# One core: local and global softmax sums as neighbours on TensorE, a fourth add of exponentials on GpSimd, and a new order table

## The chip, the cores and the metric

The kernel runs on one core of a Trainium2 chip. The metric is device time in microseconds, the median of several executions. PE is TensorE (PEld its weight loads), DVE is VectorE, ACT is ScalarE, POOL is GpSimd, SP issues DMAs.

## What is computed

A residual block over x of 2 x 8192 tokens by 512. It is normalised, projected to q, k and v for 16 heads of 32, and each query attends twice: to its local window of 64 keys, and to every 64th key of its batch (128 global keys). The two softmax results are added, projected, normalised and added to x. Then follows a second layer whose 512 x 512 matrix is worked out from a sparse spectrum, normalised and added again.

```python
qkv = (x @ w_qkv).reshape(B, N, 3, H, Dh)
logits = einsum('bnqhd,bnkhd->bhnqk', qb, kn) * scale       # keys of 3 windows around a block
logits = where(valid, logits, NEG)                          # -32 <= key - query <= 31
out_local = einsum('bhnqk,bnkhd->bnqhd', softmax(logits), vn)
lg = einsum('bnhd,bghd->bhng', q, k[:, ::W]) * scale
out_global = einsum('bhng,bghd->bnhd', softmax(lg), v[:, ::W])
out = (out_local + out_global) @ w_out + b_out
x = x + layernorm(out);  x = x + layernorm(real(ifft(fft(layernorm(x)) @ w)) + bias)
```

## The kernel before

The first phase (about a third of the time) makes q, k and v and the second layer's matrix. The second phase is a pipeline of 128 steps. A step `s` is one chunk of 512 queries and one group of four heads, so four steps make a chunk of tokens. In a step PE does, under these names:

- `max` (8 pairs of matmuls, L1111): scores from which DVE takes the row maxima (`maxr`, L1007; joined by `maxc`, L1017 to L1020); ACT fills their PSUM bank again with the mask (`seed`, L962). `mt` (L1121) transposes the maxima, and they go back by DMA as rows of the query stack.
- `loc` (8 pairs, L1133), `last` (L1143, the last 64 keys of the chunk) and `glob` (4, L1152): the scores again with the maxima taken off, into the two banks `ps_sc`; ACT takes their exponentials (L933, L940, L946). POOL masks the local ones in two passes for each of four key tiles (`locm`, L883 and L886), and the last keys' (`lastm`, L889).
- `ol` (L1167, L1170): local exponentials times values, four heads side by side in 32-column tiles of the array, into PSUM bank `ps_os`. `oc` on ACT copies it out.
- `sl` (L1186): the local softmax sums, by a matmul with a matrix of ones. A query column can get keys of two neighbouring tiles, so POOL first adds these where they overlap (`sadd`, L893, three a step), and `sl` runs four groups of four heads: 192 columns, 192 columns (the added ones), 128 columns, and the 64 columns of `p_last` (keys of the next chunk's edge, 64 partitions).
- `sg` (L1192): the global sums into the other half of the rows of `ps_os`; DVE then transposes `ps_os` (`sums`, L1024) and inverts it, and spreads it out (`rloc`, `rglob`, L1033). `pvgo` (L1199): global exponentials times values.
- a share of the chunk's `out` and `ffn` matmuls (L1215) and transposes `tr` (L1224), with their layer norms on DVE and POOL (`rs0` to `rs2`, L875 and L877).

The matmuls with 32-column tiles and the two transposes are plain fp32, the rest is fp32r. Every engine runs its items in program order. That order comes from tables of numbers: item `name` of step `s` stands at `PERIOD * s + offset`, all items are sorted by it, and each engine takes its own in that order, waiting on semaphores. The numbers are no times at run time; only the order that they give counts. ACT's exponential of `loc` waits for `sl` of the step before (`sl_done`), `pvgo` for DVE's transpose (`s_turned`), and the third part of `ol` for the fourth `locm`.

Of the kernel before, what the change touches and what calls it, by code (L numbers as in the profile page):

```python
# [21 lines left out]
F32 = mybir.dt.float32  # L22
# [630 lines left out]
def attention_phase(nc, x, v_d, b_out, b_ffn, common, stacks, out):  # L653

    with ExitStack() as ctx:
# [70 lines left out]
        def at_least(eng, s, n):  # L726
# [3 lines left out]

        PERIOD = 16.5
        STEP = {
            "max": (-24.372, -24.443, -17.457, -16.494, -14.783, -19.669, -14.65, -11.428),
            "maxr": (-22.062, -23.735, -17.887, -15.761, -20.864, -13.317, -12.389, -10.81),
            "seed": (-27.861, -23.856, -15.651, -20.132, -14.487, -12.524, -8.36, -1.966),
            "maxc": (-9.904,),
            "mt": (-8.17,),
            "x_mt": (-7.789,),
            "loc": (0.847, 1.259, 1.445, 5.277, 1.584, 4.812, 10.1, 10.414),
            "x_loc": (5.038, 3.297, 1.239, 4.532, 1.974, 9.777, 3.433, 8.956),  # L740
            "locm": (4.363, 2.995, 7.078, 11.037),
            "sadd": (4.613, 13.682, 11.307),
            "last": (4.882,),
            "x_last": (8.223,),
            "lastm": (5.505,),
            "glob": (6.183, 11.975, 7.166, 13.419),
            "x_glob": (16.404, 10.401, 5.594, 6.424),
            "ol": (14.033, 13.563, 14.113),
            "oc": (16.127,),
            "sl": (17.694,),  # L750
            "sg": (17.911,),
            "sums": (19.618,),
            "pvgo": (21.448,),
            "rglob": (21.162,),
            "ogm": (23.645,),
            "rloc": (20.665,),
            "olm": (21.594,),
            "osum": (25.997,),
        }
        BY_GROUP = {  # L760
            "ot": (50.7, 28.42, 45.746, 14.118),
            "otl": (53.185, 27.844, 37.238, 32.356),
        }
        TILE = {
            "out": (23.041, 21.305, 24.153, 22.556, 32.588, 28.022, 27.217, 27.949, 40.453, 39.05, 41.896, 35.968, 42.451, 45.411, 40.17, 44.177),
            "outa": (24.178, 32.38, 39.666, 46.206),
            "outs": (26.18, 36.087, 43.22, 47.902),
            "rs0": (35.584, 27.466, 50.9, 43.784),
            "x1": (29.059, 37.637, 44.069, 51.019),
            "x1s": (29.855, 37.995, 47.034, 55.156),  # L770
            "rs1": (41.755, 33.697, 51.9, 54.124),
            "x1n": (33.895, 45.165, 52.763, 59.748),
            "tr": (40.996, 48.411, 57.83, 64.768),
            "x_tr": (37.041, 48.379, 57.584, 60.74),
            "trl": (40.961, 48.59, 57.292, 65.635),
            "ffn": (56.275, 51.23, 56.716, 48.902, 58.624, 59.685, 61.157, 58.733, 68.241, 65.46, 73.496, 72.963, 76.644, 79.037, 76.65, 82.47),
            "ffna": (56.181, 63.299, 73.349, 83.836),
            "ffns": (79.299, 67.951, 84.667, 80.943),
            "rs2": (72.875, 81.982, 91.045, 81.147),
            "za": (77.179, 83.469, 93.936, 86.7),  # L780
        }
# [31 lines left out]
        with nc.Block() as block:  # L813
# [53 lines left out]
            def _(pool):  # L867
                for g in range(EARLY, GROUPS):
                    stacks.set_keys(pool, g)

                def rstd(k, c, i):
# [7 lines left out]
                def item(name, s, i):  # L879
# [7 lines left out]
                    if name == "lastm":  # L887
                        pool.wait_ge(sc_exped, unit(s, "last", 0) + 1)
                        pool.affine_select(p_last[:], p_last[:], [[0, 4], [1, WIN]], ALU.is_ge, 0.0,  # L889
                                           base=-1, channel_multiplier=-1).then_inc(last_masked, 1)  # L890
# [29 lines left out]
            def _(act):  # L920
# [6 lines left out]
                def item(name, s, i):  # L927
# [8 lines left out]
                    if name == "x_last":  # L936
                        n = unit(s, "last", 0)
                        act.wait_ge(sc_scored, n + 1)
                        at_least(act, sl_done, s)
                        nc.scalar.activation(p_last[:].rearrange("p h n -> p (h n)"), ps_sc[n % 2][0:WIN, 0:4 * WIN],  # L940
                                             ACT.Exp, scale=SCALE).then_inc(sc_exped, 1)
# [137 lines left out]
            def _(pe):  # L1079
# [22 lines left out]
                def item(name, s, i):  # L1102
# [51 lines left out]
                    if name == "ol":  # L1154
# [3 lines left out]
                        for tile in O_PARTS[i]:  # L1158
# [4 lines left out]
                            for h in range(4):  # L1163
                                rows, head = slice(h * DH, (h + 1) * DH), slice(h * DH, (h + 1) * DH)
                                if tile < 4:
                                    x0, w = (0, P) if tile == 0 else (P * tile - WIN, MW)
                                    last = nc.tensor.matmul(ps_os[rows, x0:x0 + w], vw[s % V_BUFS][:, tile, head], p_loc[:, tile, h, MW - w:MW],  # L1167
                                                            start=tile == 0, stop=False, skip_group_check=True)
                                else:
                                    last = nc.tensor.matmul(ps_os[rows, CHUNK - WIN:CHUNK], vl[s % V_BUFS][:, head], p_last[:, h, :],  # L1170
                                                            start=False, stop=True, skip_group_check=True)
# [92 lines left out]
```

## Time and profile before

| what | before |
|---|---|
| time, median of 3 runs | 3414.16 us (3412.81 to 3414.69) |
| the profiled execution's own time | 3419.38 us |
| its span | 3417.6 us |
| busy PE / DVE / ACT / POOL over the span | 98% / 73% / 58% / 56% |
| mean granted TensorE clock | 0.987 |

The share of busy time is the union of an engine's instructions; a matmul's recorded duration includes its way through the array, so the cost of a matmul is better read as the distance from its start to the start of what follows. DVE and POOL have low averages only because the first phase uses them little.

### The profile page before, as it was taken

The numbers are of one execution on the slowest core, as the hardware profiler recorded it, in microseconds if no ns is written. First come the engines' busy times: TensorE is split into PE (matmuls) and PEld (weight loads), VectorE is DVE, ScalarE is ACT, GpSimd is POOL, SyncE is SP. The second block draws the span as 40 slices with busy tenths as digits, with TensorE's granted clock in tenths as the row PEclk, the third lists the DMA queues.
The fourth block names the chain that finished last, engine by engine and source line by source line (L and its number), as shares of the span: only waits on it lengthen the run. The fifth ranks groups of instructions, "written<-read, shape, count | busy, mean of one in ns | idle before, by whom it ended". The sixth has DMA issues, their size and how long they took to land.

```text
span 3417.6 us, 72834 instructions
## 1 busy us (share of the span) xinstructions
PE 3338.3 (98%) x24916; PEld 2508.1 (73%) x24916; DVE 2491.0 (73%) x4425; ACT 1993.9 (58%) x3876; POOL 1915.6 (56%) x2961
## 2 busy tenths in 40 slices
PE   8999999999999699999999999999999999999997
PEld 6888888888888467777777777777777777777775
DVE  4444544445444578988898888988898889888986
ACT  2222322222222567777777777777777777777772
POOL 0000000000000378888788878888888878887885
PEclk9999999999999689999999999999999999999999
DMA  7778778787788656766667666776676666766651
GB/s 186 234 207 242 220 215 239 209 239 223 207 240 239 140 107 142 161 148 142 142 146 160 138 138 144 165 159 139 142 161 148 142 142 149 159 140 137 144 133 38
DMA packets 538325, 572.77 MB, mean 168 GB/s; under 512 B 55752, under 2 KB 354344, under 8 KB 538024
## 3 DMA queue, kind: packets, MB, share of 16 engines
q1 hardware_dynamic: 457992, 533.97, 62.6%
q10 hardware_dynamic: 79744, 34.70, 5.7%
q8 instruction: 176, 2.88, 0.4%
q14 instruction: 125, 1.02, 0.1%
q0 software_dynamic: 288, 0.20, 0.1%
HBM read 330.98 MB, written 203.23 MB: 156 GB/s over the span
## 4 chain that ended last, share of the span: by engine, by line
PE 58%; DVE 5%; POOL 2%; issue 1%; ACT 1%; ACTq 0%; POOLq 0%; DVEq 0%
PE ps_misc L1215 18%; PE ps_mx L1111 9%; PE ps_sc L1133 7%; PE ps_os L1167 5%; PE ps_os L1186 5%; PE ps_os L1192 4%; PE ps_sc L1152 3%; PE ps_os L1199 3%; PE ps_sc L1224 2%; DVE qk L1007 1%; PE ps_os L1170 1%; DVE bnb L989 1%; DVE r_loc L1033 1%; PE ps_sc L1121 1%; DVE r_glob L1033 1%
## 5 line engine op out<-in xcount | busy, mean ns | idle before, releaser
L1007 DVE TENSOR_REDUCE qk<-ps_mx 128x10 f32<-128x640 f32 x1024 | 809.4, 805 | 130.3 <-PE ps_mx L1111 119.1
L962 ACT ACTIVATE ps_mx<-mask 128x640 f32<-128x640 bf16 x1022 | 715.1, 706 | 124.3 <-DVE qk L1007 113.1
L520 PE MATMUL po<-ht_hi,w_both 128*128 128x512 f32 x2048 | 639.0, 391 | 1.5 <-ACT ht_hi L302 1.5
L933 ACT ACTIVATE qk<-ps_sc 128x384 f32<-128x384 f32 (+1 forms) x1024 | 443.4, 459 | 298.0 <-PE ps_sc L1133 242.6
L520 PEld LDWEIGHTS po<-ht_hi,w_both 128*128 128x128 f32 x2048 | 385.3, 188 | 86.3 <-issue 4.1
L883 POOL TENSOR_SCALAR_AFFINE_SELECT qk<-qk 128x512 f32<-128x512 f32 (+1 forms) x512 | 317.6, 620 | 233.1 <-ACT qk L933 228.0
L520 PE MATMUL po<-ht_lo,w_both 128*128 128x512 f32 x1024 | 399.2, 390 | 0.0
L886 POOL TENSOR_SCALAR_AFFINE_SELECT qk<-qk 128x512 f32<-128x512 f32 x512 | 335.3, 655 | 35.0
L524 PE MATMUL po<-w_both,ht_hi 128*128 128x512 f32 x1024 | 320.6, 389 | 1.3 <-DVE w_both L371 1.3
L946 ACT ACTIVATE v<-ps_sc 128x512 f32<-128x512 f32 x512 | 297.0, 593 | 33.3 <-PE ps_sc L1152 33.3
L893 POOL TENSOR_TENSOR qk<-qk 128x256 f32<-128x256 f32 x384 | 290.8, 767 | 10.7
L333 ACT ACTIVATE o_hi<-po 128x512 fp32r<-128x512 f32 x128 | 71.4, 599 | 351.7 <-PE po L524 238.5
L333 ACT ACTIVATE qk<-po 128x512 fp32r<-128x512 f32 x128 | 71.2, 599 | 350.4 <-PE po L524 142.1
L989 DVE BATCH_NORM_STATS2 bnb<-xb 128x6 f32<-128x512 f32 x384 | 258.9, 674 | 2.3
L439 DVE TENSOR_TENSOR o_lo<-po,o_hi 128x512 fp32r<-128x512 f32 x128 | 81.0, 679 | 244.8 <-ACT o_hi L333 244.8
L273 POOL CAST kg_hi<-o_hi 128x32 f32 (+1 forms) x16 | 8.2, 510 | 429.1 <-DVE o_lo L439 429.1
L439 DVE TENSOR_TENSOR o_lo<-po,qk 128x512 fp32r<-128x512 f32 x128 | 80.5, 677 | 221.2 <-ACT qk L333 221.2
L273 POOL CAST kg_hi<-qk 128x32 f32 (+1 forms) x16 | 8.5, 531 | 414.4 <-DVE o_lo L439 393.3
L1111 PE MATMUL ps_mx<-ks,w_both 97*128 97x320 f32 x1024 | 235.8, 333 | 1.5 <-ACT ps_mx L962 1.4
L877 POOL TENSOR_TENSOR rsb<-veb,mhalf_b 128x1 f32<-128x1 f32 x384 | 219.4, 571 | 31.9
L524 PEld LDWEIGHTS po<-w_both,ht_hi 128*128 128x128 f32 x1024 | 192.2, 188 | 41.6 <-DVE w_both L371 1.7
L1111 PEld LDWEIGHTS ps_mx<-ks,w_both 97*128 97x128 f32 x1024 | 164.3, 192 | 79.1 <-ACT ps_mx L962 56.9
(159 smaller groups left out, 7843.0 us busy)
## 6 DMA issues: line engine op xcount, KB each, us to landing
xb<-in_L_attn_x SPq DMA_DIRECT2D x256, 256.0 KB, 6.3
w_both<-q_hi_d SPq DMA_DIRECT2D x256, 256.0 KB
q_lo_d<-o_lo SPq DMA_DIRECT2D x32, 1024.0 KB, 8.6
k_lo_d<-o_lo SPq DMA_DIRECT2D x32, 1024.0 KB, 10.1
w_both<-q_lo_d SPq DMA_DIRECT2D x128, 256.0 KB
vw<-v_d SPq DMA_DIRECT2D x128, 256.0 KB, 5.0
out<-xb SPq DMA_DIRECT2D x128, 256.0 KB, 3.2
bt<-at ACTq DMA_DIRECT2D x496, 64.0 KB, 6.0
```

The costliest lines, as they stand in the source:

```text
L520: last = nc.tensor.matmul(po[bank(o, u)][:], wa[:, k, o * P:(o + 1) * P], ha[u][:, k, :], start=start, stop=stop)
L524: last = nc.tensor.matmul(po[bank(o, u)][:], ha[u][:, k, t * P:(t + 1) * P], wa[:, k, 2 * D:3 * D], start=start, stop=stop)
L883: pool.affine_select(early, early, [[0, 4], [1, WIN if i == 0 else P]], ALU.is_ge, 0.0, base=WIN - 1 if i == 0 else -1, channel_multiplier ...
L886: pool.affine_select(late, late, [[0, 4], [-1, P]], ALU.is_ge, 0.0, base=0, channel_multiplier=1).then_inc(loc_masked, 1)
L893: pool.tensor_tensor(p_sum[:, i, :, :], p_loc[:, i, :, P:MW], p_loc[:, i + 1, :, 0:WIN], ALU.add).then_inc(s_added, 1)
L933: nc.scalar.activation(p_loc[:, tile, 2 * hp:2 * hp + 2, lo:MW], ps_sc[n % 2][:, 0:2 * MW].rearrange("p (h n) -> p h n", h=2)[:, :, lo:MW] ...
L946: nc.scalar.activation(p_glob[:, i, :], ps_sc[n % 2][:], ACT.Exp, scale=SCALE).then_inc(sc_exped, 1)
L962: nc.scalar.activation(ps_mx[u % 2][:, :, 0:MWG], mask[:, turn:turn + 1, :].to_broadcast([P, 2, MWG]), ACT.Copy).then_inc(seeded, 1)
L989: nc.vector.bn_stats(bn[k][:, i, :], src).then_inc(bn_done[k], 1)
L1007: nc.vector.tensor_reduce(mb[s % 2][:, heads, tile, :], ps_mx[u % 2][:, :, 0:MWG].rearrange("p h (b n) -> p h b n", n=WIN), axis=AX.X, op= ...
L1111: last = nc.tensor.matmul(ps_mx[u % 2][:, n, 0:MWG], qs[g][0:ROWS_MAX, 2 * pair + n, tile * P:(tile + 1) * P], ks[g][0:ROWS_MAX, 2 * pair ...
L1215: last = nc.tensor.matmul(ps_misc[:], pick(a), w[:, k, :], start=k == 0 and n == 0, stop=k == KT - 1 and n == 2)
```

## The change

POOL gets a fourth add a step: the last tile's upper half plus `p_last`. For that `p_last` gets 128 partitions, whose upper 64 are set to zero once, and `p_sum` a fourth block; the small buffers that lay behind it move to a tensor of their own. `sl` becomes two groups of 256 columns (the lower and the upper halves of all four query tiles) and waits for the four adds alone. `sg` stands directly behind `sl`. All numbers of the order table are new; of these a few are shown. (The norms' small buffers are also joined into one tensor, and two reads of `p_last` name its first 64 partitions.)

```diff
--- before.py
+++ after.py
@@ -668,15 +668,15 @@
         qk_rest = qk0[:].rearrange("p a n -> p (a n)")[:, 16 * MW:]
-        p_sum = qk_rest[:, 0:12 * WIN].bitcast(F32).rearrange("p (i h n) -> p i h n", i=3, h=4)
+        p_sum = qk_rest[:, 0:16 * WIN].bitcast(F32).rearrange("p (i h n) -> p i h n", i=4, h=4)
...
-        p_last = sb("p_last", [WIN, 4, WIN], F32)
+        p_last = sb("p_last", [P, 4, WIN], F32)
         blocks, joined = 4 * TILES * (MWG // WIN), 8 * TILES
-        small = qk_rest[:, 12 * WIN:12 * WIN + 2 * (blocks + joined)].bitcast(F32)
+        small = sb("small", [P, 2 * (blocks + joined)], F32)[:]
...
@@ -728,56 +728,56 @@
-        PERIOD = 16.5
+        PERIOD = 16.2
         STEP = {
...
-            "sadd": (4.613, 13.682, 11.307),
+            "sadd": (11.647, 15.853, 15.494, 8.939),
...
-            "sl": (17.694,),
-            "sg": (17.911,),
+            "sl": (17.479,),
...
+            "sg": (17.48,),
...
@@ -867,6 +867,10 @@
                 for g in range(EARLY, GROUPS):
                     stacks.set_keys(pool, g)
+                for g in range(EARLY, GROUPS):
+                    pool.wait_ge(stacks.k_made[g], 1)
+                pool.memset(p_last[WIN:P], 0.0).then_inc(rest_zeroed, 1)
+                pool.wait_ge(rest_zeroed, 1)
@@ -886,11 +890,16 @@
                     if name == "sadd":
-                        pool.wait_ge(loc_masked, 4 * s + i + 2)
-                        pool.tensor_tensor(p_sum[:, i, :, :], p_loc[:, i, :, P:MW], p_loc[:, i + 1, :, 0:WIN], ALU.add).then_inc(s_added, 1)
+                        if i < 3:
+                            pool.wait_ge(loc_masked, 4 * s + i + 2)
+                            pool.tensor_tensor(p_sum[:, i, :, :], p_loc[:, i, :, P:MW], p_loc[:, i + 1, :, 0:WIN], ALU.add).then_inc(s_added, 1)
+                        else:
+                            pool.wait_ge(loc_masked, 4 * s + 4)
+                            pool.wait_ge(last_masked, s + 1)
+                            pool.tensor_tensor(p_sum[:, i, :, :], p_loc[:, i, :, P:MW], p_last[:], ALU.add).then_inc(s_added, 1)
@@ -1167,23 +1176,17 @@
                     if name == "sl":
                         pe.wait_ge(o_copied, s + 1)
-                        pe.wait_ge(s_added, 3 * s + 3)
-                        pe.wait_ge(loc_masked, 4 * s + 4)
-                        pe.wait_ge(last_masked, s + 1)
+                        pe.wait_ge(s_added, 4 * s + 4)
                         halves = ps_os[:].rearrange("p (t b n) -> p t b n", b=2, n=WIN)
-                        for n, (sums, windows) in enumerate(((halves[:, 0:3, 0, :], p_loc[:, 0:3, :, WIN:P]),
-                                                             (halves[:, 0:3, 1, :], p_sum[:]),
-                                                             (ps_os[:, CHUNK - P:CHUNK], p_loc[:, 3, :, WIN:MW]),
-                                                             (ps_os[:, CHUNK - WIN:CHUNK], p_last[:]))):
+                        for n, windows in enumerate((p_loc[:, :, :, WIN:P], p_sum[:])):
                             for h in range(4):
-                                window = windows[:, :, h, :] if len(windows.shape) == 4 else windows[:, h, :]
-                                last = nc.tensor.matmul(sums[h * DH:(h + 1) * DH], ones[0:windows.shape[0], 0, :], window,
+                                last = nc.tensor.matmul(halves[h * DH:(h + 1) * DH, :, n, :], ones[:, 0, :], windows[:, :, h, :],
                                                         start=n == 0, stop=False, skip_group_check=True)
                         last.then_inc(sl_done, 1)
```

On PE, around the sums of one step in the steady part. `ps_os<-qk,ones` is `sl`, `ps_os<-v,ones` is `sg`, `ps_sc<-w_both` is `loc`, `ps_mx` is `max`. Before:

```order
L1111 MATMUL ps_mx<-o_lo,w_both 128x320 x2
L1133 MATMUL ps_sc<-w_both 128x128 x2
L1186 MATMUL ps_os<-qk,ones 32x3x64 x8
L1186 MATMUL ps_os<-qk,ones 32x128 x4
L1186 MATMUL ps_os<-p_last,ones 32x64 x4
L1133 MATMUL ps_sc<-w_both 128x128 x2
L1192 MATMUL ps_os<-v,ones 32x512 x4
L1133 MATMUL ps_sc<-w_both 128x192 x4
```

and of the change:

```order
L1142 MATMUL ps_sc<-w_both,o_lo 128x128 x2
L1189 MATMUL ps_os<-qk,ones 32x4x64 x8
L1195 MATMUL ps_os<-v,ones 32x512 x4
L1142 MATMUL ps_sc<-w_both,o_lo 128x128 x2
L1120 MATMUL ps_mx<-ks,w_both 128x320 x4
L1142 MATMUL ps_sc<-w_both,o_lo 128x192 x4
L1202 MATMUL ps_os<-v,w_both 32x512 x4
```

The pair of `loc` that stood between the two sums now stands behind both, and two pairs of `max` stand between it and the next four `loc`; `pvgo` (the last row) follows these. In all, PE's second phase leaves its fp32 matmuls for fp32r ones 644 times before and 575 times after: 127 fewer through the joined sums, and some 60 more because 60 of the `tr` no longer stand right behind `ol`.

On POOL, in the same kind of step, from the fourth `locm` on (`qk<-qk 128x256` is a `sadd`). Before:

```order
L883 AFFINE_SELECT qk<-qk 128x4x128
L886 AFFINE_SELECT qk<-qk 128x4x128
L893 TENSOR_TENSOR qk<-qk 128x256 x2
L875 TENSOR_SCALAR veb<-mvb 128x1
L877 TENSOR_TENSOR rsb<-veb,mhalf_b 128x1
L904 TENSOR_TENSOR ot_lo<-o_loc,ot_hi 128x512
```

and of the change:

```order
L898 TENSOR_TENSOR qk<-qk 128x256
L887 AFFINE_SELECT qk<-qk 128x4x128
L890 AFFINE_SELECT qk<-qk 128x4x128
L898 TENSOR_TENSOR qk<-qk 128x256
L902 TENSOR_TENSOR qk<-qk,p_last 128x256
L879 TENSOR_SCALAR ln_small<-mvb 128x1
```

Of the two adds behind the fourth mask one now stands ahead of it, and the new one is the last, with `sl` waiting for it.

## Rows read from the trace of the kernel before

**Rows 1.** Windows: busy us (instructions) of PE, PEld, DVE, ACT, POOL; clock; DMA share, GB/s

```profile
2000.00:2500.00 500.00, 497.42 (x4540) 356.96 (x4538) 445.31 (x781) 382.41 (x750) 413.12 (x637) 1.00 0.69 152
```

**Rows 2.** Line L1192 (`sg`): count, duration ns min/median/max, first and last start

```profile
L1192 PE MATMUL ps_os<-v,ones x1024: 592/617/1062, 1161.0 to 3364.4; 128*32 128x512 f32 x171
```

**Rows 3.** Timeline of PE around the sums: start us, duration us

```profile
2010.75 0.56 PE L1111 MATMUL ps_mx<-ks,w_both 97*128 97x320 f32 x2
2011.15 0.40 PE L1215 MATMUL ps_misc<-ht_hi,ot_hi 128*128 128x512 f32 x1
...
2011.84 0.46 PE L1111 MATMUL ps_mx<-ks,w_both 97*128 97x320 f32 x2
2012.14 0.34 PE L1133 MATMUL ps_sc<-w_both,ks 99*128 99x128 f32 x2
2012.41 1.08 PE L1186 MATMUL ps_os<-qk,ones 128*32 128x192 f32 x24
2013.41 0.32 PE L1186 MATMUL ps_os<-p_last,ones 64*32 64x64 f32 x8
2013.66 0.44 PE L1133 MATMUL ps_sc<-w_both,ks 99*128 99x128 f32 x2
2014.03 1.07 PE L1192 MATMUL ps_os<-v,ones 128*32 128x512 f32 x8
2015.02 0.69 PE L1133 MATMUL ps_sc<-w_both,ks 99*128 99x192 f32 x4
2015.56 0.77 PE L1111 MATMUL ps_mx<-ks,w_both 97*128 97x320 f32 x4
```

**Rows 4.** Weight loads of `ol`: the first 24 and the last 8, twice

```profile
2009.01 0.70 PEld L1167 LDWEIGHTS ps_os<-qk,vw 128*32 128x32 f32 x24 [0.27 <-issue]
2010.04 0.16 PEld L1167 LDWEIGHTS ps_os<-qk,vw 128*32 128x32 f32 x8 [0.34 <-POOL qk L886]
...
2061.76 0.70 PEld L1167 LDWEIGHTS ps_os<-qk,vw 128*32 128x32 f32 x24 [0.28 <-issue]
2062.64 0.16 PEld L1167 LDWEIGHTS ps_os<-qk,vw 128*32 128x32 f32 x8 [0.17 <-POOL qk L886]
```

**Rows 5.** Timeline of PE, earlier in the step: among fp32r work, and ahead of `ol`

```profile
2005.62 0.59 PE L1133 MATMUL ps_sc<-w_both,o_lo 99*128 99x192 f32 x4
2006.04 0.41 PE L1215 MATMUL ps_misc<-ht_hi,ot_hi 128*128 128x512 f32 x1
...
2008.16 0.40 PE L1152 MATMUL ps_sc<-w_both,o_lo 99*128 99x512 f32 x1
2008.39 0.46 PE L1111 MATMUL ps_mx<-ks,w_both 97*128 97x320 f32 x2
2008.69 0.39 PE L1152 MATMUL ps_sc<-w_both,o_lo 99*128 99x512 f32 x1
```

**Rows 6.** Timeline of PE, `tr` behind `ol`

```profile
2028.76 0.66 PE L1224 MATMUL ps_sc<-ident,xb 128*128 128x128 f32 x4
2029.17 0.55 PE L1111 MATMUL ps_mx<-w_both 97*128 97x320 f32 x2
2029.56 0.40 PE L1215 MATMUL ps_misc<-ht_hi,w_both 128*128 128x512 f32 x1
```

**Rows 7.** POOL's fourth mask of a step, from the timeline

```profile
2009.36 0.63 POOL L886 TENSOR_SCALAR_AFFINE_SELECT qk<-qk 128x512 f32<-128x512 f32 x1
```

**Rows 8.** Two lines by themselves: duration ns min/median/max

```profile
L893 POOL TENSOR_TENSOR qk<-qk x364: 722/732/1179, 1255.9 to 3353.2; 128x256 f32<-128x256 f32 x182
...
L1072 DVE SCALAR_TENSOR_TENSOR xb<-xb,rsb x120: 705/814/1739, 1297.1 to 3325.3; 128x512 f32<-128x512 f32 x120
```

**Rows 9.** Waits, second phase: total us, times, longest

```profile
PEld ps_os L1167 <- POOL qk L886: 38.1, 118, 0.5
...
PE ps_sc L1121 <- DVE qk L1020: 10.8, 31, 0.7
```

**Rows 10.** DVE's transpose of the sums, from the timeline

```profile
2015.16 0.72 DVE L1024 STREAM_TRANSPOSE r_loc<-ps_os 128x512 f32<-128x512 f32 x1 [0.83 <-PE ps_os L1192]
```

More of the change, by code:

```diff
@@ L690, in attention_phase @@
         mv = [sb(f"mvb{s}", [P, TILES, 2], F32) for s in range(3)]
-        ve = [sb(f"veb{s}", [P, TILES], F32) for s in range(3)]
-        rs = [sb(f"rsb{s}", [P, TILES], F32) for s in range(3)]
-        nm = sb("nmb", [P, TILES], F32)
+        ln_small = sb("ln_small", [P, 7, TILES], F32)
+        ve, rs, nm = [ln_small[:, s, :] for s in range(3)], [ln_small[:, 3 + s, :] for s in range(3)], ln_small[:, 6, :]
         ps_mx = [pb(f"ps_mx{b}", [P, 2, 512]) for b in range(2)]
@@ L729, in at_least @@
                 eng.wait_ge(s, n)
-        PERIOD = 16.5
+        PERIOD = 16.2
         STEP = {
[L733 to L741, printed above, removed]
-            "sadd": (4.613, 13.682, 11.307),
[L743 to L749, printed above, removed]
-            "sl": (17.694,),
-            "sg": (17.911,),
[L752 to L758, printed above, removed]
@@ new lines, in attention_phase @@
+            "max": (-22.973, -23.083, -15.972, -16.628, -14.326, -17.22, -14.155, -11.779),
+            "maxr": (-22.311, -19.382, -16.644, -17.707, -22.258, -13.723, -10.173, -12.806),
+            "seed": (-27.909, -21.612, -13.06, -21.226, -13.222, -10.253, -7.789, -0.058),
+            "maxc": (-9.955,),
+            "mt": (-7.27,),
+            "x_mt": (-6.711,),
+            "loc": (1.266, 2.114, 2.835, 5.662, 1.315, 2.274, 10.719, 10.704),
+            "x_loc": (4.205, 3.241, 3.329, 5.933, 3.897, 15.001, 10.514, 9.508),
@@ new lines, in attention_phase @@
+            "locm": (4.658, 9.475, 5.273, 11.717),
+            "sadd": (11.647, 15.853, 15.494, 8.939),
+            "last": (2.648,),
+            "x_last": (7.09,),
+            "lastm": (9.258,),
+            "glob": (6.857, 14.929, 5.767, 15.117),
+            "x_glob": (14.538, 9.424, 4.656, 7.492),
+            "ol": (15.45, 15.342, 15.601),
+            "oc": (17.408,),
+            "sl": (17.479,),
+            "sums": (18.279,),
+            "pvgo": (18.713,),
+            "rglob": (20.388,),
@@ L759, in attention_phase @@
+            "ogm": (23.319,),
+            "rloc": (18.943,),
+            "olm": (22.597,),
+            "osum": (26.525,),
+            "sg": (17.48,),
         }
         BY_GROUP = {
-            "ot": (50.7, 28.42, 45.746, 14.118),
-            "otl": (53.185, 27.844, 37.238, 32.356),
+            "ot": (51.511, 28.196, 46.751, 18.998),
+            "otl": (50.34, 30.06, 37.661, 32.769),
         }
         TILE = {
-            "out": (23.041, 21.305, 24.153, 22.556, 32.588, 28.022, 27.217, 27.949, 40.453, 39.05, 41.896, 35.968, 42.451, 45.411, 40.17, 44.177),
@@ L766, in attention_phase @@
[L766 to L780, printed above, removed]
+            "out": (23.599, 20.491, 20.183, 22.378, 31.386, 29.662, 27.719, 28.443, 40.447, 38.809, 41.916, 35.438, 46.927, 46.895, 42.657, 38.672),
@@ new lines, in attention_phase @@
+            "outa": (25.391, 29.738, 38.966, 43.469),
+            "outs": (25.573, 34.059, 42.992, 46.239),
+            "rs0": (36.909, 27.655, 49.56, 45.901),
+            "x1": (28.362, 36.683, 46.292, 50.393),
+            "x1s": (30.556, 38.867, 47.116, 58.485),
+            "rs1": (42.62, 33.253, 49.788, 58.943),
+            "x1n": (39.097, 46.871, 52.003, 60.222),
+            "tr": (41.191, 48.251, 57.398, 64.709),
+            "x_tr": (51.385, 41.612, 66.663, 56.474),
+            "trl": (40.997, 49.931, 58.67, 64.968),
@@ L781, in attention_phase @@
+            "ffn": (56.003, 54.903, 48.528, 51.62, 58.747, 60.766, 72.451, 60.681, 71.637, 79.715, 58.873, 70.207, 69.051, 75.721, 76.648, 79.55),
+            "ffna": (58.47, 60.134, 73.868, 78.72),
+            "ffns": (58.962, 69.064, 74.832, 79.36),
+            "rs2": (82.577, 83.188, 80.759, 68.475),
+            "za": (77.293, 86.781, 91.146, 80.599),
         }
@@ L888, in item @@
                         pool.wait_ge(sc_exped, unit(s, "last", 0) + 1)
-                        pool.affine_select(p_last[:], p_last[:], [[0, 4], [1, WIN]], ALU.is_ge, 0.0,
+                        pool.affine_select(p_last[0:WIN], p_last[0:WIN], [[0, 4], [1, WIN]], ALU.is_ge, 0.0,
                                            base=-1, channel_multiplier=-1).then_inc(last_masked, 1)
                     if name == "sadd":
-                        pool.wait_ge(loc_masked, 4 * s + i + 2)
-                        pool.tensor_tensor(p_sum[:, i, :, :], p_loc[:, i, :, P:MW], p_loc[:, i + 1, :, 0:WIN], ALU.add).then_inc(s_added, 1)
+                        if i < 3:
[5 more added lines that the diff above has]
+                            pool.tensor_tensor(p_sum[:, i, :, :], p_loc[:, i, :, P:MW], p_last[:], ALU.add).then_inc(s_added, 1)
                     if name == "olm":
@@ L939, in item @@
                         at_least(act, sl_done, s)
-                        nc.scalar.activation(p_last[:].rearrange("p h n -> p (h n)"), ps_sc[n % 2][0:WIN, 0:4 * WIN],
+                        nc.scalar.activation(p_last[0:WIN].rearrange("p h n -> p (h n)"), ps_sc[n % 2][0:WIN, 0:4 * WIN],
                                              ACT.Exp, scale=SCALE).then_inc(sc_exped, 1)
@@ L1169, in item @@
                                 else:
-                                    last = nc.tensor.matmul(ps_os[rows, CHUNK - WIN:CHUNK], vl[s % V_BUFS][:, head], p_last[:, h, :],
+                                    last = nc.tensor.matmul(ps_os[rows, CHUNK - WIN:CHUNK], vl[s % V_BUFS][:, head], p_last[0:WIN, h, :],
                                                             start=False, stop=True, skip_group_check=True)
```

1 line of the change is left out of this document (added).

## The prediction

> **What bounds the kernel now.** I read the windows first. In a steady stretch of 500 us PE is busy 497.42, DVE 445.31, ACT 382.41 and POOL 413.12, at the full granted clock [rows 1]. So in the second phase PE is the bound, with DVE and POOL not far behind, and every bit of PE time that is taken out should show as long as those two keep up. The length of a step comes from the first and last `sg`: 1024 instructions are 128 steps of 8, and (3364.4 - 1161.0) / 127 = 17.35 us [rows 2].
>
> Next the timeline of PE, read from start to start. Two things are to be seen. First, what each group of `sl` costs: its 24 instructions of 192, 192 and 128 columns (512 in sum) take 2013.41 - 2012.41 = 1.00, and the 8 of `p_last` with only 64 columns take another 0.25 [rows 3]. Second, changing between the 32-column fp32 matmuls and the 128-column fp32r ones costs time on both sides. A pair of `max` takes 0.40 behind such a run and 0.30 elsewhere [rows 3]; four `loc` of 192 columns take 0.54 behind `sg` [rows 3] and 0.42 among fp32r work [rows 5]; a `glob` takes 0.23 in general and 2009.01 - 2008.69 = 0.32 when `ol` follows it [rows 4, 5]. So going in costs about 0.10 and coming out about 0.11.
>
> Last the waits. The fourth part of `ol`'s tiles is regularly held by POOL's fourth mask (38.1 us in 118 times [rows 9]): the mask ends at 2009.36 + 0.63 = 2009.99 and the loads go at 2010.04 [rows 4, 7]. How much of that is real? Tiles of 512 columns stand ahead of it; once it came 0.88 behind `ol`'s start and at other times 1.03 [rows 4], so the true loss is up to 0.15 a step.
>
> **The change part by part.** All terms are us per step, on PE.
>
> 1. The `p_last` group goes: -0.25 [rows 3].
> 2. The remaining two groups have 256 + 256 = 512 columns, as `sl`'s first 24 instructions (1.00) and as `sg` (2015.02 - 2014.03 = 0.99) [rows 3]. But both of these are followed by another shape of tile, and some of the 1.00 is the array running empty. Where 512 columns in the same shape are followed by more of the same, the next can start after 0.88 [rows 4]. With `sg` right behind, I take `sl` at 0.88: -0.12. The bounds are 0 (nothing saved, by `sg`'s row) and 0.15 (the 0.88 was itself cut off by a wait for POOL).
> 3. The pair of `loc` between the sums. It costs 2014.03 - 2013.66 = 0.37 there, while the same pair that only goes in costs 2012.41 - 2012.14 = 0.27 [rows 3]. Now it stands behind both sums and only comes out, so it loses the 0.10 of going in, and the four `loc` that stood behind `sg` lose the 0.12 of coming out (0.54 to 0.42). Together -0.22.
> 4. `tr`. Behind `ol`, it let one exit serve both. 60 of the 128 now stand alone among fp32r work. A pair of `max` behind `tr` takes 2029.56 - 2029.17 = 0.39 [rows 6], against 0.30 undisturbed [rows 3]. So +0.09 x 60 / 128 = +0.04.
> 5. The new add on POOL is like L893: 0.73 in the median, 1.18 at most [rows 8]. POOL's load rises from 413.12 / 500 = 83% to (0.826 x 17.35 + 0.73) / 16.8 = 90%. Not on PE's path if it ends in time. Behind the fourth mask come two adds (1.46). PE meanwhile has the last 192 columns of `ol` (an estimate by the 0.88 for 512 columns, plus an exit: 0.33 + 0.11 = 0.44), 0.25 for `p_last`'s part of it (by `sl`'s like group), two pairs of `max` (0.40 + 0.30) and the pair of `loc` (0.27) [rows 3, 4]: 1.66. So the cover is 0.2 even if the mask ends just in time as now. That the first `sadd` now stands ahead of the mask makes the mask 0.73 later on POOL; three `out` matmuls that in one step of four stood behind `ol` now stand ahead of it, and DVE's norms that POOL waits for stand earlier in the order. I cost term 5 at nothing; if its cover is gone it is up to 0.73 a step.
> 6. `pvgo` waits for DVE's transpose, which starts 0.14 after PE leaves `sg` and takes 0.72 [rows 3, 10]. Between `sg` and `pvgo` there now stand a pair of `loc`, four `max` and four `loc`, 0.27 + 0.61 + 0.42 = 1.30 (the 0.61 an estimate, twice 0.30). 0.4 is left, so nothing. Without this cover PE would stand 0.9 a step.
> 7. The new order elsewhere: PE has the same matmuls otherwise. The start (one memset on POOL) happens once, and the semaphores that `sl` no longer names had been reached: nothing.
>
> The sum is -0.25 - 0.12 - 0.22 + 0.04 = -0.55 a step, or 70 us over 128 steps. The profiled execution took 3419.4 us (span 3417.6 and 1.8 around it), which gives 3349; the median of the runs is 5.2 lower, so in its terms **3344**.
>
> A page has a rule for terms 2 and 3. The Trainium skill, "TensorEngine Tiling (Array Packing)", Key Properties, says that a change of tiling mode, not merely of tile, drains TensorE. By it two drains a step go; without it, terms 2 and 3 would be nothing and the sum 27 us.
>
> **The rivals.**
>
> *The gain is partly given back to waits.* DVE is at 89% and would be at 445.31 / 500 x 17.35 / 16.8 = 92%, POOL at 90%, and each is waited for once or twice a step already: by `ol` [rows 9], and by `mt` (31 waits of up to 0.7 for the joined maxima [rows 9]). Where these loops and not PE set the pace, the matmul saved is idle time gained. For it: the third part of `ol` is held in nearly every step. Against it: the two sums and the `loc` between them lie on that very loop (from mask to `ol` to `sg` to DVE's transpose), so it gets shorter too. If 0.25 of the 0.55 stays lost: 3414 - 38 = 3376.
>
> *The run of fp32 brings nothing.* If the cost of changing is bound to the shapes and not to the neighbours, only terms 1 and 4 are left: 0.21 x 128 = 27 us, 3387. Rows 3 and 5 speak against it in three places.
>
> *Waits vanish too.* If the true loss of up to 0.15 at `ol` [rows 4] and some of that at `mt` go with the new order, another 20 to 25 us: 3320.
>
> *Slower: POOL's last add comes too late for `sl`.* `sl` now waits for a chain mask, add, add. L893 can take 1.18 [rows 8]. If both did in every step, the chain would take 2.36 against 1.68 of cover, plus the norms' POOL work that in one step of four stands between (rs and the low part of `ot`), about 0.3 a step spread out: PE waits 1.0, and loses 0.45 net, 57 us: 3471. The median of 0.73 is against it. It decides from a mean wait of 0.55 ahead of `sl`.
>
> A rule that speaks for this one: the Trainium skill, "SBUF — State Buffer", the section on the two separate sides, says that DVE operations with two SBUF inputs and GpSimd ones share a port pair that is locked for a whole instruction. What the trace shows is DVE's L1072 with 705 at least, 814 in the median and 1739 at most [rows 8]. Going by the rows, such a line meets POOL's work more often in proportion to POOL's load (83% to 90%), and as its median excess is 0.11 the addition is 0.01 an instruction, two a step: hidden in DVE's idle time. The rule gives no other number.
>
> **How the numbers follow.** PE stays the bound and gains 45 to 90 us: 0.60. Partly given back (15 to 45 us): 0.22. No gain from the run: 0.06. Waits vanish too (over 90 us): 0.07. Slower: 0.03. Left, about no change: 0.02. The bounds of term 2 alone give 55 to 74 us. The range should leave out 0.2: below, the half of the waits that vanish; above, the upper part of the part given back. That is 3315 to 3378. Change within 0.2% (7 us) is about what this kernel's runs cannot tell from none; faster 0.95, same 0.02, slower 0.03.
>
> **What would show it.** In the profile after: `sl` 16 instructions with `sg` starting 0.85 to 1.00 behind it, no 0.25 piece between; the pair of `loc` behind `sg` near 0.27 and the four `loc` near 0.42; the step at 16.8 instead of 17.35; POOL near 90%. It is wrong if PE's idle share grows, with `sl` waiting for the new add, `pvgo` for the transpose, or `mt` or `ol` for DVE and POOL longer than before.

## The result and the profile after

The changed kernel takes 3364.66 us in the median of 4 runs (3360.81 to 3368.82), the kernel before 3414.43 (4 runs): a ratio of 0.985, 95% interval 0.9838 to 0.9862, or 50 us less. That is in the stated range of 3315 to 3378. The forecast was 3344, so about 20 us of the 70 expected are missing.

The step got shorter by what the total did. Line L1195 (`sg`) of the profile after, with count, durations and first and last start:

```profile
L1195 PE MATMUL ps_os<-v,ones x1024: 592/592/1062, 1161.4 to 3313.6; 128*32 128x512 f32 x171
```

(3313.6 - 1161.4) / 127 = 16.95 us a step, against 17.35 [rows 2]: 0.40 less, where the sum said 0.55. The first `sg` starts where it did before, at 1161.0 then and 1161.4 now, so the whole gain lies in the steps behind it.

The windows of a steady stretch after (busy us of PE, PEld, DVE, ACT, POOL; clock; DMA):

```profile
2000.00:2500.00 500.00, 491.62 (x4172) 359.51 (x4171) 458.12 (x802) 391.40 (x770) 447.79 (x684) 1.00 0.69 151
```

Against [rows 1] PE has fallen from 497.42 to 491.62: it stands idle more. Per step that is 17.35 x 497.42 / 500 = 17.26 us busy and 0.09 idle before, and 16.95 x 491.62 / 500 = 16.66 busy and 0.28 idle now. So PE's work shrank by 0.60 us, a little more than the 0.55 of the sum, and 0.19 of it came back as idle time. DVE is at 92% and POOL at 90%, as worked out. The chain that ended last, on the page of the kernel after, says who takes part now:

```profile
PE 30%; POOL 29%; DVE 3%; issue 2%; ACT 1%; ACTq 0%; POOLq 0%; DVEq 0%
```

On the page before, POOL had 2% of that chain and PE 58%. PE's own waits between 1200 and 3300 us (total us, times, longest), first the kernel before, with all of its waits above 1 us, then the kernel after, with those above 2:

```profile
PE ps_sc L1121 <- DVE qk L1020: 10.8, 31, 0.7
PE ps_sc L1152 <- ACT qk L933: 3.1, 4, 1.0
```

```profile
PE ps_os L1176 <- POOL qk L890: 15.3, 30, 0.5
PE ps_os L1189 <- POOL qk L902: 14.7, 31, 1.4
PE ps_sc L1161 <- ACT qk L942: 4.1, 4, 2.1
```

Two waits for POOL are new, 30 us together, each in about one step of four: `ol` for the fourth mask (L890) and `sl` for the fourth add (L902). The wait of `mt` for the joined maxima (10.8) is nearly gone. Here is one of the steps in which `sl` waits, on PE:

```profile
2008.36 0.56 PE L1120 MATMUL ps_mx<-w_both 97*128 97x320 f32 x2
...
2010.19 0.33 PE L1142 MATMUL ps_sc<-w_both,ks 99*128 99x128 f32 x2
2010.96 1.07 PE L1189 MATMUL ps_os<-qk,ones 128*32 128x256 f32 x16 [0.44 <-POOL qk L902]
2011.83 1.07 PE L1195 MATMUL ps_os<-v,ones 128*32 128x512 f32 x8
2012.82 0.44 PE L1142 MATMUL ps_sc<-w_both,ks 99*128 99x128 f32 x2
2013.10 0.80 PE L1120 MATMUL ps_mx<-w_both 97*128 97x320 f32 x4
2013.74 0.59 PE L1142 MATMUL ps_sc<-w_both,ks 99*128 99x192 f32 x4
2014.26 0.64 PE L1202 MATMUL ps_os<-v,o_lo 128*32 128x512 f32 x4
```

`sl` to `sg` is 0.87 (taken at 0.88), the pair of `loc` behind them 0.28 (0.27), and the group of `p_last` is gone. The next four `loc` take 0.52 and not the 0.42 of the sum, because `pvgo` follows them directly; in the kernel before it was `last` that stood ahead of `pvgo` and took longer for it (0.30, 0.26 now). `pvgo` follows without a wait. But `sl` starts 0.77 behind the start of a pair of `loc` that needs 0.27: it is held for half a microsecond by the fourth add. POOL and DVE in the same place:

```profile
2006.14 0.64 POOL L890 TENSOR_SCALAR_AFFINE_SELECT qk<-qk 128x512 f32<-128x512 f32 x1
2006.86 0.22 POOL L879 TENSOR_SCALAR ln_small<-mvb 128x1 f32<-128x1 f32 x1
2007.16 0.57 POOL L881 TENSOR_TENSOR ln_small<-ln_small,mhalf_b 128x1 f32<-128x1 f32 x1
2007.70 1.28 POOL L913 TENSOR_TENSOR ot_lo<-o_loc,ot_hi 128x512 fp32r<-128x512 f32 x1
2008.94 1.18 POOL L898 TENSOR_TENSOR qk<-qk 128x256 f32<-128x256 f32 x1
2010.09 0.73 POOL L902 TENSOR_TENSOR qk<-qk,p_last 128x256 f32<-128x256 f32 x1
```

```profile
2008.45 1.08 DVE L1062 SCALAR_TENSOR_TENSOR xb<-xb,ln_small 128x512 f32<-128x512 f32 x1
```

The third add takes 1.18 instead of 0.73, and DVE's operation with two SBUF inputs, which starts just before it, 1.08 instead of 0.73. The mask (L890) had ended at 2006.78; 2.1 us of work for the layer norms and `ot` stand between it and the third add, so the chain ahead of `sl` has nothing to spare, and the 0.45 by which the add is drawn out is about what `sl` waits. In one other step of four it is worse: there the second add and the first pass of the fourth mask are drawn out, both ahead of `ol`'s third part. POOL, and under it PE's weight loads:

```profile
2055.27 1.17 POOL L898 TENSOR_TENSOR qk<-qk 128x256 f32<-128x256 f32 x1
2056.39 1.09 POOL L887 TENSOR_SCALAR_AFFINE_SELECT qk<-qk 128x512 f32<-128x512 f32 x1
2057.55 0.64 POOL L890 TENSOR_SCALAR_AFFINE_SELECT qk<-qk 128x512 f32<-128x512 f32 x1
```

```profile
2056.65 0.70 PEld L1176 LDWEIGHTS ps_os<-qk,vw 128*32 128x32 f32 x24 [0.36 <-issue]
2058.24 0.16 PEld L1176 LDWEIGHTS ps_os<-qk,vw 128*32 128x32 f32 x8 [0.89 <-POOL qk L890]
```

The third part follows 1.59 behind `ol`'s start, where 0.88 would do [rows 4]: 0.71 lost in this step. The add and the first pass are drawn out by 0.44 and 0.45, together more than that.

### The profile page after: what moved, and what is told of

The parts are those of the page before. It is cut to its first block, busy times and chain, and to the rows that moved or that the text cites. A ratio compares the mean times of both kernels' runs of the same rounds, so it can differ in the third digit from the quotient of the medians.

```text
span 3363.3 us, 68869 instructions
## 1 busy us (share of the span) xinstructions
PE 3259.7 (97%) x22868; PEld 2473.6 (74%) x22868; DVE 2504.9 (74%) x4425; ACT 1991.2 (59%) x3876; POOL 2019.3 (60%) x3090
## 4 chain that ended last, share of the span: by engine, by line
PE 30%; POOL 29%; DVE 3%; issue 2%; ACT 1%; ACTq 0%; POOLq 0%; DVEq 0%
PE ps_misc L1218 9%; POOL qk L887 5%; POOL qk L890 5%; POOL qk L898 5%; PE ps_mx L1120 4%; PE ps_sc L1142 4%; POOL ot_lo L913 3%; PE ps_os L1189 3%; POOL o_loc L906 3%; PE ps_os L1195 3%; POOL o_loc L910 2%; POOL ln_small L881 2%; PE ps_os L1176 2%; PE ps_os L1202 2%; PE ps_sc L1161 1%
## 5 line engine op out<-in xcount | busy, mean ns | idle before, releaser
L1016 DVE TENSOR_REDUCE small<-ps_mx 128x10 f32<-128x640 f32 x1024 | 803.4, 803 | 141.2 <-PE ps_mx L1120 137.3
L887 POOL TENSOR_SCALAR_AFFINE_SELECT qk<-qk 128x512 f32<-128x512 f32 (+1 forms) x512 | 325.0, 635 | 135.5 <-ACT qk L942 133.8
L890 POOL TENSOR_SCALAR_AFFINE_SELECT qk<-qk 128x512 f32<-128x512 f32 x512 | 325.2, 635 | 35.0
L898 POOL TENSOR_TENSOR qk<-qk 128x256 f32<-128x256 f32 x384 | 323.4, 842 | 8.2
L955 ACT ACTIVATE v<-ps_sc 128x512 f32<-128x512 f32 x512 | 289.4, 592 | 7.3 <-PE ps_sc L1161 7.3
L881 POOL TENSOR_TENSOR ln_small<-ln_small,mhalf_b 128x1 f32<-128x1 f32 x384 | 220.2, 573 | 32.0
L1120 PE MATMUL ps_mx<-ks,w_both 97*128 97x320 f32 x1024 | 220.9, 328 | 2.7 <-ACT ps_mx L971 2.7
L520 PEld LDWEIGHTS po<-ht_lo,w_both 128*128 128x128 f32 x1024 | 192.9, 188 | 39.3
```

Of the source, the lines that this page charges most:

```text
L520: last = nc.tensor.matmul(po[bank(o, u)][:], wa[:, k, o * P:(o + 1) * P], ha[u][:, k, :], start=start, stop=stop)
L881: pool.tensor_tensor(rs[k][:, i:i + 1], ve[k][:, i:i + 1], mhalf[:], ALU.pow).then_inc(rs_done[k], 1)
L887: pool.affine_select(early, early, [[0, 4], [1, WIN if i == 0 else P]], ALU.is_ge, 0.0, base=WIN - 1 if i == 0 else -1, channel_multiplier ...
L890: pool.affine_select(late, late, [[0, 4], [-1, P]], ALU.is_ge, 0.0, base=0, channel_multiplier=1).then_inc(loc_masked, 1)
L955: nc.scalar.activation(p_glob[:, i, :], ps_sc[n % 2][:], ACT.Exp, scale=SCALE).then_inc(sc_exped, 1)
L1016: nc.vector.tensor_reduce(mb[s % 2][:, heads, tile, :], ps_mx[u % 2][:, :, 0:MWG].rearrange("p h (b n) -> p h b n", n=WIN), axis=AX.X, op= ...
```

## The experiments

Each kernel was timed in five rounds (4 to 11 runs) beside the kernel before (3414.3 to 3415.6 in these rounds). All differences from the changed kernel are taken to its 3364.7. PE's busy and idle time a step are worked out as above, from the window of 2000 to 2500 us and the starts of `sg` in each run.

**1 to 3: the parts in the old order.** `e1_run_only` is the kernel before with

```diff
-            "sg": (17.911,),
+            "sg": (17.695,),
```

> The kernel before with sg moved directly behind sl and nothing else. Theory (PE bound, leaving and entering the 32-column run costs time): terms 2 and 3 alone, 0.12 + 0.22 = 0.34 us a step, 44 us: about 3371; less if the loop over POOL's masks holds it, but the run lies on that loop too. Rival (the run brings nothing, the gain is the missing p_last group): 3414.

`e2_add_only` is the changed code with the old table, the fourth add behind the third; `e3_old_order` the same with `sg` behind `sl`.

```diff
-            "sadd": (4.613, 13.682, 11.307),
+            "sadd": (4.613, 13.682, 11.307, 13.69),
```

> The changed code (fourth add, sl in two groups) in the old order, sg still behind the pair of loc, the fourth add behind the third. Theory: term 1 alone, 0.25 us a step, 32 us: about 3382. Rival (POOL is late for sl with the fourth add): 3395 to 3414, and a wait of sl for L902 in most steps.

> The changed code with both, but all other numbers of the old table. If the new table is what keeps the waits small, this is slower than the changed kernel: the third sadd and the fourth come late behind the otl and norm work, 3375 to 3390. If the new table only costs (60 exits more behind tr, sadd ahead of the fourth mask), it is faster: 3414 - 76 = 3338 to 3350.

Measured, in the order of the three expectations: 3491.8 (ratio 1.0224, interval 1.021 to 1.0238), 3442.9 (1.0083, 1.0069 to 1.0097) and 3485.5 (1.0207, 1.0193 to 1.0221). All three are slower than the kernel before, and both my theory and the rival I had set against each are off by far. PE in the first of them:

```profile
2019.77 0.32 PE L1186 MATMUL ps_os<-p_last,ones 64*32 64x64 f32 x8
2020.02 1.07 PE L1192 MATMUL ps_os<-v,ones 128*32 128x512 f32 x8
2021.01 0.69 PE L1133 MATMUL ps_sc<-w_both,o_lo 99*128 99x128 f32 x4
2021.92 0.47 PE L1133 MATMUL ps_sc<-w_both,o_lo 99*128 99x192 f32 x2 [0.22 <-ACT qk L933]
```

Six `loc` now follow `sg` without a break, and the last pair cannot start before ACT has emptied its bank (0.22 idle). That happens in nearly every step, and never in the kernel before:

```profile
PE ps_sc L1133 <- ACT qk L933: 25.8, 117, 0.2
```

It is a part only of the 77 us. Further up the same loop more is waited for, too: between 1200 and 3300 us, ACT's waits for PE's `loc` grow from 226.4 to 303.5 us and POOL's for ACT's exponentials from 185.0 to 263.5. My reading is that in the old order the pair of `loc` between the sums fed ACT during `sg`, and that the exponentials, masks and adds now all start later; no run tests it by itself. In `e2` the longest wait of PE's weight loads for ACT or POOL is

```profile
PEld ps_mx L1120 <- ACT ps_mx L971: 130.3, 153, 1.5
```

but in the kernel before the same wait is 113.9 us in 155 times over the same stretch. What is new on PE itself is `sl`'s wait for the fourth add (23.4 us in 61 times) and one of `max` for ACT (15.8 us in 30). PE's busy time falls there by 0.19 us a step and its idle time grows from 0.09 to 0.46. So term 1, which PE does gain, is more than eaten. The add's wait by itself is less than half of the 61 us between the 3382 of term 1 and the 3443 measured; why `max` waits longer was not tested.

**4: the fourth add made small.** `e4_small_add`:

```diff
-pool.tensor_tensor(p_sum[:, i, :, :], p_loc[:, i, :, P:MW], p_last[:], ALU.add)
+pool.tensor_tensor(p_sum[:, i, 0, 0:1], p_loc[:, i, 0, P:P + 1], p_last[:, 0, 0:1], ALU.add)
```

> The changed kernel in which the fourth add adds one column of one head instead of 256 columns (the rest of the last block of p_sum is left stale, so some local sums are wrong); PE, ACT, DVE and all semaphores unchanged. Theory that POOL gives back 0.15 us a step, because its work ahead of sl and of ol's third part is too long in two steps of four: 15 to 25 us faster, 3340 to 3350, and sl no longer waits for L902. Rival (POOL's waits cost nothing and the terms of PE were too large): within 3 us of 3365.

3352.3 (0.9817, 0.9803 to 0.983): 12 us faster than the changed kernel. The add falls from 0.73 to 0.19, `sl` no longer waits for it (one time), the wait of `ol`'s weight loads and matmuls for the mask falls from 43.7 to 7.5 us, and PE is busy 495.83 of 500. So both waits for POOL go with the add. The time won is less than their 30 us and a little under what was expected: `mt`'s wait for the joined maxima is back (8.1 us in 32 times), and one for ACT is new (4.0).

**5: less POOL work in another place.** `e5_less_pool`:

```diff
-pool.tensor_scalar(ve[k][:, i:i + 1], mv[k][:, i, 1:2], EPS, None, ALU.add).then_inc(ve_done[k], 1)
-pool.wait_ge(ve_done[k], n)
-pool.tensor_tensor(rs[k][:, i:i + 1], ve[k][:, i:i + 1], mhalf[:], ALU.pow).then_inc(rs_done[k], 1)
+pool.tensor_tensor(rs[k][:, i:i + 1], mv[k][:, i, 1:2], mhalf[:], ALU.pow).then_inc(rs_done[k], 1)
```

> The changed kernel without the epsilon of the three layer norms of a tile: POOL's L879 (0.26 us, 12 in a chunk) and the wait behind it are left out, all else and the order as they are. POOL's work falls by 0.8 to 1.3 us a step, at other places than in the run with the small add. Theory (POOL's total work ahead of ol and sl is what gives back): again 8 to 15 us faster, 3350 to 3357. Rival (only the fourth add itself, by its place, holds sl): 3362 to 3366.

3380.2 (0.9896, 0.9881 to 0.9911): 15.5 us slower, though POOL's busy time falls to 421.49 of 500. This overthrows "POOL's total work is what gives back". Two groups of lines show what grew, in the kernel after and then here (count | busy us, mean ns | idle before):

```profile
L1062 DVE SCALAR_TENSOR_TENSOR xb<-xb,ln_small 128x512 f32<-128x512 f32 x120 | 140.7, 1172 | 0.7 <-POOL ln_small L881 0.6
L1081 DVE SCALAR_TENSOR_TENSOR xb<-xb,ln_small 128x512 f32<-128x512 f32 x119 | 94.7, 796 | 0.0
```

```profile
L1060 DVE SCALAR_TENSOR_TENSOR xb<-xb,ln_small 128x512 f32<-128x512 f32 x117 | 157.6, 1347 | 0.0
L1079 DVE SCALAR_TENSOR_TENSOR xb<-xb,ln_small 128x512 f32<-128x512 f32 x119 | 127.5, 1072 | 0.0
```

The two DVE lines take 0.45 us a step more together, and PE, whose waits for POOL are gone, now waits for DVE's transpose ahead of `pvgo` (2 times in the kernel after). The weight loads:

```profile
PEld ps_os L1200 <- DVE r_loc L1031: 22.7, 31, 1.7
```

That the longer DVE lines cause this wait is argued from these rows, not shown. So the question became what draws these lines out (run 11).

**6, 7 and 12: the parts in the new order.** `e6_new_order_old_sums` is the code before with the new table (three of its four `sadd` numbers); `e12_order_only` the same with `sg` behind the pair of `loc`; `e7_loc_between` the changed kernel with that edit:

```diff
-            "sg": (17.48,),
+            "sg": (17.52,),
```

> The code before (sl in four groups, three adds a step) in the new order, with sg behind sl. Against the changed kernel PE has 0.25 us a step more for the group of p_last and perhaps 0.10 more, since this group's other shape now stands between sl and sg; POOL has 0.73 less. Theory of my sum: 32 to 45 us slower than the changed kernel, less the 12 that POOL gives back: 3385 to 3400. Rival (POOL's add costs as much as the group saves): near 3365.

> The changed kernel with sg one place later, behind the pair of loc, as it stood before. Theory (terms 2 and 3 are 0.12 + 0.22 us a step): 43 us slower than the changed kernel, 3408; somewhat less if loc, which then comes 0.9 us earlier, lets ACT and POOL go earlier: down to 3390. Rival (a run in one piece brings nothing): 3365 or faster.

> The code before (four groups, three adds) in the new order, with sg behind the pair of loc as before: the new table alone. Theory (by the terms of PE the table has no gain of its own, 0.04 us a step of loss through tr, and the gain comes from the sums): 3415 to 3430, slower than e6 by 0.34 less the 0.10 of the shape change, 30 to 45 us. Rival (the table alone carries the gain): 3365 to 3390.

Measured: 3387.6 (0.9917, 0.9903 to 0.993), 3419.4 (1.0017, 1.0008 to 1.0026) and 3440.8 (1.0075, 1.0062 to 1.0087). With runs 1 to 3 this makes a full table of medians:

| | sums apart, as before | sums joined |
|---|---|---|
| old order, four groups and three adds | 3414 (before) | 3492 |
| old order, two groups and four adds | 3443 | 3486 |
| new order, four groups and three adds | 3441 | 3388 |
| new order, two groups and four adds | 3419 | 3365 (after) |

In the new order joining wins 53 and 55 us; in the old one it costs 77 and 43. The new order by itself costs 26 with the old code, which is more than was expected of `e12` (3415 to 3430); with two groups and four adds it wins 24, but from a slower start. `e7` shows why joining wins more than terms 2 and 3:

```profile
2032.10 0.33 PE L1142 MATMUL ps_sc<-w_both,ks 99*128 99x128 f32 x2
2032.88 1.07 PE L1189 MATMUL ps_os<-qk,ones 128*32 128x256 f32 x16 [0.45 <-POOL qk L902]
2034.41 0.41 PE L1142 MATMUL ps_sc<-w_both,ks 99*128 99x128 f32 x2 [0.45 <-issue]
2034.74 1.07 PE L1195 MATMUL ps_os<-v,ones 128*32 128x512 f32 x8
```

In two steps of four the pair of `loc` between the sums is not ready (0.45 idle here); `sg` behind `sl` fills that time. In `e12` it is one step of four, and that wait is most of what the new order costs by itself; in the kernel before (0.3 us) and in `e6` (none) it is not there:

```profile
PE ps_sc L1133 <- issue: 21.4, 30, 0.8
```

The row names no releaser. That it is the score bank, which with `tr` ahead is free only when DVE has read it, fits the order but was not tested. `e6` has 1.01 + 0.24 + 1.00 for `sl`, `p_last` and `sg`, against 0.87 + 0.99 after: PE gains 0.39 a step by the two groups, 50 us, and the measured time shows 23. The other 27 are put down to the fourth add by subtraction. PE's waits say the same: between 1200 and 3300 us they come to 11 us in `e6`, none of them for POOL, and to 37 in the kernel after, 30 of them for POOL.

**8: an out unit behind `ol`.** `e8_out_behind_ol` changes one number of `out` from 31.386 to 32.4.

> The changed kernel with one number of the table other: in one step of four the out matmuls of index 7 stand behind ol and two max instead of ahead of ol. Theory (in that step POOL's chain of third add, fourth mask, two adds is late, 0.7 us at ol and 0.5 at sl): PE fills the wait with 0.7 us of work that it has to do anyway, at sl; ol's wait becomes longer by as much, so only what sl waited is won: 0 to 15 us, 3350 to 3364. Rival (the waits come from elsewhere): 3365 or more.

3426.4 (1.0031, 1.0019 to 1.0043): 62 us slower for a move of three matmuls in one step of four. DVE's add of that result (L1055) stands in DVE's order ahead of a row maximum, so DVE stood still until PE was past `ol`. That line's waits in this run (4.3 us in 3 times in the kernel after):

```profile
  PE ps_misc L1218: 83.8, 34
```

PE's wait of `ol` for POOL's mask, which was to be filled, grew from 15.3 to 35.6 us instead. I had looked at PE and POOL there, not at who is queued behind the consumer on DVE.

**9 and 10: the place and the dose of the adds.** `e9_mask_first` changes `"sadd": (11.647, ...)` to 11.75; `e10_add_twice` repeats the fourth add:

```diff
+pool.tensor_tensor(p_sum[:, i, :, :], p_loc[:, i, :, P:MW], p_last[:], ALU.add).then_inc(s_twice, 1)
+pool.wait_ge(s_twice, s + 1)
 pool.tensor_tensor(p_sum[:, i, :, :], p_loc[:, i, :, P:MW], p_last[:], ALU.add).then_inc(s_added, 1)
```

> The changed kernel with the second add of each step on POOL behind the fourth mask (as it was before the change) instead of ahead of it; one number of the table. Theory (in one step of four the chain add, mask, add, add is late as a whole): the wait of ol's third part (0.7 us in that step) goes, but sl waits for the same last add, so only some is won, and in the other steps three adds (2.2 us) stand between mask and sl, where PE has 1.7 to 3: 3360 to 3385. Rival (only the place of the second add holds PE): 22 us faster, 3343.

> The changed kernel with the fourth add done twice, one after the other (result unchanged): POOL has 0.73 us a step more, straight ahead of sl. In the changed kernel's trace sl starts 0.14 to 0.21 behind the last add in two steps of four (held by it) and 0.66 to 0.76 in the other two (cover of about 0.5). Theory: 0.75 us in two steps and 0.25 in the other two, 0.5 a step: 64 us slower than the changed kernel, 3425 to 3435. Rival (POOL has slack on average, its waits shift only): under 20 us slower.

3375.8 (0.9886, 0.9871 to 0.99), 11 us slower: the wait moves from `ol` to `sl`, which now waits 45.6 us in 61 times (14.7 in 31 in the kernel after). And 3451.6 (1.0109, 1.0095 to 1.0122), 87 us slower for 128 x 0.73 = 93 us of POOL work: beyond the present add there is next to no cover. I had worked out 64 us from the slack of single steps, which was too little.

**11: DVE operations with one SBUF input.** `e11_one_input`:

```diff
-nc.vector.scalar_tensor_tensor(xb[:, i, :], yb[:, i, :], rs[0][:, i:i + 1], xb[:, i, :], ALU.mult, ALU.add)
+nc.vector.transpose(xb[:, i, :], yb[:, i, :])
...
-nc.vector.scalar_tensor_tensor(yb[:, i, :], yb[:, i, :], rs[2][:, i:i + 1], xb[:, i, :], ALU.mult, ALU.add)
+nc.vector.transpose(yb[:, i, :], xb[:, i, :])
```

> The changed kernel in which the two DVE operations with two SBUF inputs (L1062 and L1081, residual and scale of the layer norms) are each replaced by a transpose with one input, which takes 0.70 us, the same as they take undisturbed; scale and residual are left out. Theory (two-input DVE operations and POOL's hold one another up): these rows fall from means of 1.17 and 0.80 to 0.70, POOL's adds (mean 0.85) and L906 (1.40) to their minimum of 0.73 and 1.27, and the waits of ol and sl for POOL shrink: 10 to 20 us faster, 3345 to 3355. Rival: durations and time as they are.

3311.1 (0.9701, 0.9688 to 0.9714): 54 us faster, where 10 to 20 were expected. This kernel leaves out the scale and residual of the layer norms, so it is a measuring device and no better kernel. The lines in this run, of POOL and of DVE:

```profile
L898 POOL TENSOR_TENSOR qk<-qk 128x256 f32<-128x256 f32 x357 | 263.1, 737 | 7.4
L887 POOL TENSOR_SCALAR_AFFINE_SELECT qk<-qk 128x512 f32<-128x512 f32 x357 | 226.5, 634 | 14.3 <-ACT qk L942 12.5
...
L1062 DVE STREAM_TRANSPOSE xb<-xb 128x512 f32<-128x512 f32 x124 | 84.8, 684 | 2.4 <-POOL ln_small L881 2.3
L1080 DVE STREAM_TRANSPOSE xb<-xb 128x512 f32<-128x512 f32 x122 | 84.3, 692 | 0.0
```

and in the kernel after:

```profile
L898 POOL TENSOR_TENSOR qk<-qk 128x256 f32<-128x256 f32 x354 | 300.5, 849 | 7.3
...
L887 POOL TENSOR_SCALAR_AFFINE_SELECT qk<-qk 128x512 f32<-128x512 f32 x354 | 250.7, 708 | 8.3 <-ACT qk L942 6.6
```

POOL's adds fall from 849 to 737 ns and its masks from 708 to 634, though nothing of POOL was changed, and the windows of the steady stretch are those of a kernel that PE alone bounds:

```profile
2000.00:2500.00 500.00, 499.69 (x4289) 369.05 (x4287) 453.79 (x816) 398.08 (x786) 433.24 (x697) 1.00 0.72 159
```

## Why the prediction was right, and where its sizes were off

The course was right: PE bounded the kernel, the sums' cost on PE fell, and the median lies in the range, with the gain of 50 us at the lower edge of the 45 to 90 that the likeliest case was to give. By its mechanism it is the second case that came, the gain partly given back to waits: PE's idle share grew from 0.5% to 1.7%, with `sl` waiting for the new add and `ol` longer for POOL, which the prediction had named as a sign of being wrong. What PE was to save came out right in sum (0.60 us a step against 0.55); what was put at nothing, the waits, cost 0.19.

- *Term 1* (the group of `p_last`, 0.25) and *term 2* (0.12 from the same shape of tile running on) hold on PE: 1.01 + 0.24 against 0.87. The Trainium skill's rule on changes of tiling mode ("TensorEngine Tiling (Array Packing)", Key Properties) agrees with this: with `p_last`'s other shape behind it the same 512 columns took 1.01.
- *Term 3* (0.22) holds for the pair of `loc` (0.28); the four `loc` took 0.52 because `pvgo` follows them, a cost that `last` had before. The test of joining by itself gave more: 55 us between `e7` and the changed kernel for the 44 of terms 2 and 3, and 53 between `e12` and `e6` for the 31 that was expected there, since `sg` also covers a wait of `loc`.
- *Term 7*, that the new order elsewhere costs nothing, was wrong as a statement on a part: the new order alone costs 26 us (`e12`), not the 5 of term 4. Most of this is the wait of the pair of `loc`, and it is gone once the sums are joined, so the 21 us too much here and the 22 us too much that joining wins in `e6` are one and the same wait. That they cancel in the sum was not foreseen. Of the eight kernels in the table only the two with the new order and the joined sums are faster than the kernel before.
- *Term 5*, the fourth add hidden at no cost, is the mis-sized one that decides. I took the chain behind the mask as two adds of 0.73 and its cover as 1.66 (in the rival it stands as 1.68, a slip). In two steps of four POOL is later: in one the norms' work and an add of 1.18 stand ahead of the last add, in the other the mask itself is late. PE's two new waits for POOL come to 30 us. Between `e6` and the changed kernel 27 of 50 us are given back, and `e4` gets 12 back by leaving most of the add out.
- *Term 6*, `pvgo`, was right: 2.6 us of waits in all, in 2 times.

By the measured parts the sum is +26 (order) - 53 (joined) - 23 (groups and add together) = -50 us.

The rival of POOL's add coming late for `sl` had its mechanism right and its weight wrong: `sl` waits 0.11 us in the mean of the steps (14.7 / 128), where 0.55 was to make the change a loss. In the old order, too, `sl` waits for the add, but that is less than half of what `e2` loses. The note on two-input DVE operations had it as 0.02 us a step at most, because I scaled the median excess of one DVE line by POOL's load. It left out that POOL's own lines are drawn out as well, and that they lie on the path. `e11` gives 54 us, 0.43 a step, for the whole of this contention and not only its growth. The Trainium skill's rule ("SBUF — State Buffer", the two separate sides: whichever starts first holds the shared pair for its whole instruction) agrees with the rows on both engines: DVE's operation started at 2008.45 while POOL was in its 1.28 (to 2008.98), and POOL's add at 2008.94 while DVE was in its 1.08 (to 2009.53), and each took some 0.4 longer than alone. That the 54 us contain nothing but this (the replaced DVE lines are also shorter at their minimum, 0.68 against 0.73) is not shown to the last microsecond. Nor was the same replacement made in the kernel before, so how much of the 54 us the change brought with it is open.

The missing 20 us, then, are 30 us of new waits for POOL, half at `ol` and half at `sl`, less the 10 that PE no longer waits for the joined maxima. What stays open is how that split would be in another order: `e5`, `e8` and `e9` show that it changes with every shift of the pipeline. No run that does all of the kernel's work was faster than the changed kernel.

## What to carry to other kernels

- In a software pipeline whose engines stand at 90% and more, price a part only in the order it will run in. The same edit (joined sums) cost 77 us in one order and won 53 in another.
- When work is moved to a helper engine, ask what it collides with and what gates the bound engine right behind it, not whether the helper has idle time. One more add of the same size cost 87 of its 93 us.
- Moving one producer later is a question to its consumer's queue: what stands behind the consumer on that engine waits as well.

## What the runs showed of the hardware that was not expected

- POOL's adds and masks and DVE's operation with two SBUF inputs draw each other out, in single cases from 0.73 to 1.18 and from 0.73 to 1.76 us; with a one-input operation in its place POOL's two lines run near their minimum in the mean (737 and 634 ns).
- 512 columns of fp32 in 32-column tiles take 1.00 us when another shape of tile follows and 0.87 when the same shape follows.
